# Maxima by query halves, spaced by TensorE's passes, in a four-layer attention kernel

## What is computed

```
xn = group_norm(x) * gn_w + gn_b
qkv = einsum('oc,bct->bot', qkv_w, xn) + qkv_b          # 8 heads: q, k, v of 32 channels
weight = softmax(einsum('bct,bcs->bts', q * scale, k * scale), axis=-1)
a = einsum('bts,bcs->bct', weight, v)
x = xn + einsum('oc,bct->bot', proj_w, a) + proj_b
```

## Time and profile before

| | us |
|---|---|
| three runs: median (lowest, highest) | 1786.18 (1785.3, 1792.4) |
| the profiled execution's own time | 1780.42 |
| its span, first to last instruction | 1778.6 |
| layers 0 and 1, and the prologue, to the first score of P0 | 613.9 |
| P0 to P14 (first score of P0 to that of P15) | 1087.0 |
| P15 and the end | 77.7 |

### The profile page before, as it was taken

One profiled execution on the slowest core, in us unless ns is written; L12 is line 12 of the kernel. 1 busy time (PEld: TensorE's weight loads), 2 busy tenths in 40 slices (PEclk: granted clock), 3 DMA queues, 4 the chain that ended last, 5 costly groups with the idle time before them and its releaser, 6 DMA issues.

```text
span 1778.6 us, 25007 instructions
## 1 busy us (share of the span) xinstructions
PE 1635.6 (92%) x8222; PEld 1004.7 (56%) x8222; DVE 1042.0 (59%) x1640; ACT 903.9 (51%) x1488; POOL 990.9 (56%) x394
## 2 busy tenths in 40 slices
PE   4888969999996899999999999999999999999987
PEld 2767758888884554554544545545455454454532
DVE  3665646455443776666765767567666576656621
ACT  3444415344341265565655666556556555555653
POOL 1222303122131187776886778678777687757785
PEclk7999989999997699999999999999999999999999
DMA  4000000000003113113031130330312303033000
GB/s 146 19 18 18 1 1 1 1 1 1 18 1 78 36 37 72 31 43 74 1 72 39 35 90 0 72 72 7 72 25 49 79 20 72 13 85 73 1 25 24
DMA packets 25085, 67.60 MB, mean 38 GB/s; under 512 B 7216, under 2 KB 9072, under 8 KB 24944
## 3 DMA queue, kind: packets, MB, share of 16 engines
q1 hardware_dynamic: 24944, 65.82, 15.1%
HBM read 7.82 MB, written 4.19 MB: 7 GB/s over the span
## 4 chain that ended last, share of the span: by engine, by line
PE 48%; DVE 8%; issue 4%; POOL 3%; DMA 2%; ACT 1%; SPq 1%; DVEq 0%; POOLq 0%; ACTq 0%
PE psO L954 12%; PE psD L89 11%; PE psD L1022 10%; PE psA L1049 7%; DVE BNS L1102 6%; PE psD L966 5%; POOL PA L1259 3%; PE psO L1049 3%; DMA QS<-MROW 2%; ACT PR L1212 1%; DVE sums_turned L1079 1%; DVE A L1083 1%; SPq L1286 1%; SPq L1288 0%; DVE A L1085 0%
## 5 line engine op out<-in xcount | busy, mean ns | idle before, releaser
L1102 DVE TENSOR_REDUCE BNS<-psD 128x1 f32<-128x512 f32 x1024 | 631.1, 681 | 180.7 <-PE psD L1022 180.6
L1259 POOL TENSOR_TENSOR PA<-PA,PR 128x2048 f32<-128x2048 f32 x128 | 585.7, 4576 | 14.2 <-ACT PR L1212 2.0
L1212 ACT ACTIVATE PR<-psA 128x512 f32<-128x512 f32 x688 | 396.3, 607 | 324.7 <-PE psA L1049 281.6
L1022 PE MATMUL psD<-KS,QS 96*128 96x512 f32 x1024 | 420.6, 445 | 17.3 <-DMA QS<-SL 10.8
L1049 PE MATMUL psA<-QS,KS 97*128 97x512 f32 x688 | 294.9, 437 | 40.6 <-DMA QS<-MROW 19.3
L1022 PEld LDWEIGHTS psD<-KS,QS 96*128 96x128 f32 x1024 | 198.9, 194 | 139.5 <-DVE BNS L1102 92.3
L1212 ACT ACTIVATE PR<-psO 128x512 f32<-128x512 f32 x336 | 203.8, 607 | 143.7 <-PE psO L1049 141.4
L680 POOL TENSOR_SCALAR P<-P,RS 128x1024 f32<-128x1024 f32 x64 | 71.8, 1122 | 360.1 <-DVE RS L398 360.1
L954 PE MATMUL psO<-PR,V 128*32 128x512 f32 x2048 | 246.4, 598 | 0.0
L1049 PEld LDWEIGHTS psA<-QS,KS 97*128 97x128 f32 x688 | 128.7, 190 | 179.6 <-issue 97.6
L1259 POOL TENSOR_TENSOR PA<-PR 128x2048 f32<-128x2048 f32 x32 | 146.4, 4576 | 146.1 <-PE psD L1022 127.6
(11 more groups left out here) (146 smaller groups left out, 2062.9 us busy)
## 6 DMA issues: line engine op xcount, KB each, us to landing
KS<-SH SPq DMA_DIRECT2D x128, 128.0 KB, 2.4
QS<-SH SPq DMA_DIRECT2D x128, 128.0 KB, 2.4
KS<-SL SPq DMA_DIRECT2D x64, 128.0 KB, 2.4
QS<-SL SPq DMA_DIRECT2D x64, 128.0 KB, 2.4
X<-x SPq DMA_DIRECT2D x4, 1024.0 KB, 9.2
out<-X SPq DMA_DIRECT2D x4, 1024.0 KB, 4.5
XN<-w SPq DMA_DIRECT2D x2, 768.0 KB, 8.5
KH<-KL SPq DMA_DIRECT2D x8, 128.0 KB, 2.3
```

The costliest lines, as they stand in the source:

```text
L1022: mm = e.matmul(full, QS[0:STACK, g, q, tile * PART:(tile + 1) * PART], KS[0:STACK, g, q, h * HALF:(h + 1) * HALF], start=True, stop=True)
L1102: top = e.tensor_reduce(MXH[:, h, q, tile:tile + 1], full, AX.X, ALU.max)
L1212: e.activation(PR[:, J % 4, (s % QUADH) * HALF:(s % QUADH + 1) * HALF], score_bank(s, p), ACT.Exp, scale=scale).then_inc(exp_done, 1)
L1259: e.tensor_tensor(PA[:, :], PR[:, (J - 1) % 4, :] if j == 1 else PA[:, :], PR[:, J % 4, :], ALU.add).then_inc(sum_done, 1)
```

## The change

- Maxima are made by **query halves**. `m` are the 32 of queries 0 to 511 of group G; `a` ("late") are the 32 of queries 512 to 1023. Six late ones of group G are made in the phase before it (`EARLY`), the other 26 in its own phase. `T` and `t` turn a half each, three units behind its last maximum (`LAG`). Step 0 waits for the first row, step 32 for the second. The prologue makes 38 maxima in place of 64, and P15 makes 26 where it had none.
- The times of the 64 maxima follow from TensorE's **passes**: `side_units` adds up what each step costs (`PASSES`) and places a maximum at every 64th part of the sum, so most now come as two to four in a step that has other long work, and steps with the score alone come two or three running.
- `WEIGH` moves its pairs to steps 11, 18, 26, 34, the sums `z` go from 34.9 and 2.9 to 36 and 4. `v`, `w`, `K`, `Q`, `p` move (`SIDE_AT`). The `x` operations go from steps 15 and 17 to 32 to 36, statistics are spread over steps 8.5 to 14.5, and the group means ride on `t`. GpSimd works out the factors and `input_low` between its two series of adds, and the low parts behind the second one.
- `QS` is laid out by query halves, so a copy to it has two runs of 2 KB for one of 4 KB. In the SP queue the stacks of group 1 stand ahead of the first row of group 0.

```
-        M_AT = (6, 58)
-        HOLES = [(35, 38)]
-        XN_AT = 12
-        HALVES_AT = {"v": (0, 1), "w": (3.5, 5), "K": (28, 29.3), "Q": (30.6, 31.9), "p": (14.5, 17.5, 20.5, 23.5),
-                     "z": (34.9, 2.9)}
+        EARLY = 6
+        LAG = 3
+        XN_AT = (32, 34, 36, 36)
+        BN_AT = (8.5, 10.5, 12.5, 14.5)
+        SIDE_AT = [{"v": (14.5, 21), "w": (23.5, 29.5), "K": (45, 47), "Q": (52.5, 54.5)},
+                   {"v": (5, 6.2), "w": (8.2, 9.4), "K": (45, 47), "Q": (52.5, 54.5), "p": (14.5, 29.5, 21, 23.5)}]
+        WEIGH = [(0, 11), (1, 11), (2, 18), (3, 18), (4, 26), (5, 26), (6, 34), (7, 34)]
+        PASSES = {"K": 6, "Q": 6, "v": 6, "w": 2, "z": 12, "p": 8}
+        Z_AT = (36, 4)
+        FIRST_AT = {"k": (0.1, 0.2), "q": (0.3, 0.4), "v": (1, 1.1), "w": (2, 2.1), "K": (8, 10), "Q": (12, 14)}
+        W3_AT = 28
...
+                load = [1] * STEPS
+                for u, ats in halves.items():
+                    for at in ats:
+                        load[-int(-at // 1)] += PASSES[u]
+                for _, at in WEIGH:
+                    for h in range(2):
+                        load[(at + STEPS // 2 * h) % STEPS] += QUADH
+                passed = [0] + list(accumulate(load))
+                for i in range(4 * ROWS):
+                    share = (i + 0.5) * passed[-1] / (4 * ROWS)
+                    s = [p <= share for p in passed].index(False) - 1
+                    ats.append(s - 1 + (share - passed[s]) / load[s])
...
-                        wait(e, row_dma, (P + 1) * 16)
                         for s in range(STEPS):
+                            if s % HALF_STEPS == 0:
+                                wait(e, row_dma, (2 * P + h + 1) * 16)
...
+                    def maxima(G, h):
+                        e.wait_ge(vec_free, units_taken(G + h, "Tt"[h]))
+                        e.dma_start(QS[STACK:STACK + 1, G % 2, h, :, :].rearrange("p q n -> p (q n)").bitcast(F32),
+                                    MROW[:, :].bitcast(F32)).then_inc(row_dma, 16)
+                    stack(0)
+                    stack(1)
+                    maxima(0, 0)
+                    for P in range(NGRP):
+                        maxima(P, 1)
...
+                        if P + 1 < NGRP:
+                            maxima(P + 1, 0)
+                        if P + 2 < NGRP:
+                            stack(P + 2)
```

More of the change, by code:

```diff
@@ L1 @@
 from contextlib import ExitStack
+from itertools import accumulate
 import concourse.bass as bass
@@ new lines, in side_units @@
+        def side_units(g, first=False, last=False):
+            early, late = (0 if last else EARLY), (0 if first and g == 0 else 2 * ROWS - EARLY)
+            tiles = ([("late", a) for a in range(2 * ROWS - late, 2 * ROWS)]
+                     + [("first", a) for a in range(0 if last else 2 * ROWS)] + [("late", a) for a in range(early)])
+            if first and g == 0:
+                halves, step = FIRST_AT, 1
+                ats = [6 + i for i in range(len(tiles))]
+            else:
+                halves, step = dict({} if last else SIDE_AT[g]), STEPS / (4 * ROWS)
+                halves["z"] = Z_AT
+                if first:
+                    del halves["p"]
+                load = [1] * STEPS
[6 more added lines that the diff above has]
+                passed = [0] + list(accumulate(load))
+                ats = []
+                for i in range(4 * ROWS):
+                    share = (i + 0.5) * passed[-1] / (4 * ROWS)
+                    s = [p <= share for p in passed].index(False) - 1
+                    ats.append(s - 1 + (share - passed[s]) / load[s])
+                step = 1
+            units = [(u, at, i) for u, at_halves in halves.items() for i, at in enumerate(at_halves)]
+            if first and g:
+                units = [x for x in units if x[0] != "z" or x[2] == 0]
+            for n, ((kind, a), at) in enumerate(zip(tiles, ats)):
+                units.append(("a" if kind == "late" else "m", at, a))
+                if a == 2 * ROWS - 1:
+                    units.append(("t" if kind == "late" else "T", ats[min(n + LAG, len(ats) - 1)] + 0.01, 0))
@@ L857, in units_taken @@
         def units_taken(G, u):
-            place, r = (G, None) if G < 2 else (2 + G % 2, G // 2 - 1)
+            place, r = (G, None) if G < 2 else (2 + G % 2, G // 2 - 1) if G < NGRP else (4, None)
             units = UNITS[place]
-            return base_of("vector", place, r) + taken(units, [x[0] for x in units].index(u) + 1, "vector")
-        WEIGH = [(0, 13), (1, 13), (2, 18), (3, 18), (4, 26), (5, 26), (6, 33), (7, 33)]
+            names = [x[0] for x in units]
+            return base_of("vector", place, r) + taken(units, len(names) - names[::-1].index(u), "vector")
         PIECES = NT - 1
@@ L1109, in take @@
                             take_half(full, p ^ i, i)
-                        elif u == "T":
-                            wait(e, row_dma, G * 16)
-                            e.tensor_scalar(MROW[:, :], full[0:QUADH * NT, 0:PART], -1.0, None,
+                        elif u in "tT":
+                            if u == "t" and norm is not None:
+                                e.tensor_copy(MV[:, :, :].rearrange("p t k -> p (t k)"), full[:, PART:PART + 2 * CT])
+                            wait(e, row_dma, (2 * G if u == "T" else 2 * P + 1) * 16)
+                            e.tensor_scalar(MROW[:, :], full[0:ROWS, 0:PART], -1.0, None,
                                             ALU.mult).then_inc(vec_free, 1)
@@ L1222, in factors @@
                     def factors(norm, place, r, layer):
-                        names = [u for u, _, _ in UNITS[place]]
-                        after = len(names) - names[::-1].index("s")
+                        after = [u for u, _, _ in UNITS[place]].index("t") + 1
                         e.wait_ge(vec_free, base_of("vector", place, r) + taken(UNITS[place], after, "vector"))
@@ L1242, in phase @@
                     def phase(P, p, G, g, place, r, layers, proj=None, norm=None, norm_b=None):
-                        if norm is not None and P is not None:
-                            squares(e, norm)
-                            factors(norm, place, r, layers[2])
                         if P is None:
@@ L1261, in phase @@
                                 if norm is not None and h == 0 and j == 3:
-                                    input_low(norm, norm_b, layers[2])
-                                if layers[0] != layers[1] and h == 0 and j == 3:
+                                    squares(e, norm)
+                            if norm is not None and h == 0:
+                                factors(norm, place, r, layers[2])
+                                input_low(norm, norm_b, layers[2])
+                                if layers[0] != layers[1]:
                                     e.wait_ge(w3_high, 1)
@@ L1277, in _, with stack @@
                     e.dma_start(WP[:, :, :], wp_dram[2]).then_inc(wp_loaded[2], 16)
-                    for G in range(NGRP):
+                    def stack(G):
                         g = G % 2
```

156 lines of the change are left out of this document (71 added, 85 removed).

## The result

The changed kernel takes 1793.1 us (median of 20 runs, 1790.4 to 1796.9), the kernel before 1785.3 (20 runs, 1777.0 to 1792.4). The ratio is 1.0044 with a 95% interval of 1.0033 to 1.0056: slower, by 7.8 us. The execution under the profiler took 1793.9 us with a span of 1792.1, where the one of before took 1780.4 with 1778.6. So the two profiles stand 13.5 us apart, the medians 7.8.

A forecast was written before the change was run, and what follows sets the result against it. TensorE was taken as the bound, losing 6.2 us per odd and 5.6 per even phase to row and VectorE waits. P0 +3.2, P1 to P14 +1.9, prologue -6.7, last phase +1.0: -0.6 on 1780.4; median 1786, range 1765 to 1810.

The forecast's parts named there:

- ScalarE's pace: Steps without side work run at exp's 0.49 us, costing TensorE 2.6 us in an odd phase, 2.7 in an even.
- The start: Prologue: fewer maxima, but K's eviction and stack(1)'s copies delay it; P0 starts at 607.2 instead of 613.9, -6.7 us.
- the loop entries: Three re-entries of the two loops keep their instruction-issue gap, 4.3 us each with half clock, 12.9 in all.
- Evictions: Maxima four units behind v, w, K or Q wait for ScalarE to empty banks: 3.0 us odd, 2.6 even.
- The second row: Odd phases, score 32: the row turned by t comes late, 1.25 us lost; hidden in even phases.
- P0: First phase: exp 32 waits for GpSimd's factors without output quarters as cover; 70.0 us against 66.8, +3.2.
- P15: Last phase, GpSimd-bound: 26 maxima put its first add 1.5 us later, one more ready score returns 0.5; +1.0 us.
- (a): Whole kernel: no change, within 9 us, as the forecast's own sum says; chance 0.40.
- (b): Eviction waits overlap ScalarE's pace and t's row comes in time, so faster: 1740 to 1775 us; chance 0.27.
- (c): GpSimd's adds, chained with exp, become the bound; even phases lose 3 us each with the next odd: 1807; chance 0.18.
- (d): More small waits in ten places of 14 phases, +35, or SP's queue holds t's row: 1805 to 1820; chance 0.11.
- (e): ScalarE-paced stretches bring the 0.95 clock everywhere, 3 us a phase, +45: 1830 us; chance 0.04.

The follow-up runs named there:

- e1_pieces: Changed kernel with only the pieces v, w, K and Q moved to other steps; 1767.0 us, 0.9907 of the kernel before.
- e6_half_exp: Changed kernel with exp over 256 of the 512 columns of each score, so its output differs; 1757.7 us, 0.9840 of the kernel before.
- e3_uniform: Changed kernel with one maximum per step instead of counting passes, and LAG = 1; 1783.8 us, 0.9986 of the kernel before.
- e5_ends: Changed kernel with P0's input operations four steps later and P15's second sum at step 3, maxima one per 0.8 step; 1796.7 us, 1.0070 of before.
- e4_start: Changed kernel with the prologue reordered: K and Q of group 1 behind T, first row's copy ahead of stack(1); 1781.1 us, 0.9976 of before.
- e10_holes: e3_uniform with six light steps behind the sums without a maximum and six weighting-pair steps with two; 1771.8 us, 0.9927 of before.
- e7_all: Changed kernel with the edits of e1_pieces (w placed differently), e4_start, P0 and P15 (maxima per 0.9 step), plus EARLY 7; 1747.1 us, 0.9793 of before.
- e8_steps: Changed kernel with maxima spaced by steps with six holes, EARLY 7, LAG 2, and v, w, K, Q moved; 1734.9 us, 0.9715 of before.
- e9_best: e8_steps plus the edits of the prologue, P0 and P15 (maxima one per 0.9 step); 1717.6 us, 0.9620 of before.

## Why the prediction was wrong

I forecast no change, and it is slower by 0.44%. The step that failed is the size of three terms of the sum: *ScalarE's pace* in the odd phase (2.6 us forecast, about 4.2 in P5), the eviction waits of P0 (put at nothing) and the first add of P15 (1.5 us later forecast, 2.9 measured). The mechanisms were those foreseen.

*The start* (607.2, measured 608.2) and *the loop entries* (three of 3.3 to 3.9 us of issue; with the half clock behind them some 14 us in place of 12.9) were near. In the start, each split copy to `QS` holds the queue 0.67 us where it was 0.64, about half a us for the 12 of a stack; I had taken nothing. At the three entries the gap stayed though the row no longer waits, so the row was not its cause. That it is the fetch of the branch's instructions is argued and not shown: the trace gives no releaser. The Trainium skill, page "Runtime: NRT & Kernel Launch", section "Instruction fetch mechanics", says that a taken branch whose target is outside the fetched window stalls until its page arrives; the three entries of 3.3 to 3.9 us fit that. That one entry of e1_pieces shows 0.17 with the same branch is left open. P6's weights (0.8) cost next to nothing: P6 takes 75.3, the even phases beside it 75.1 and 75.2.

*Evictions* (3.0 odd, 2.6 even) were about right. The brackets of P5 say 2.0 us (0.65, 0.50, 0.18, 0.66), but from start to start these four places lose 0.81, 0.66, 0.34 and 0.81: 2.6. In P6 it is 1.8; of the waits that I listed for it ahead of e1_pieces, the 0.34 is not one for an eviction. *The second row* (1.25) costs 0.84, counted the same way. *ScalarE's pace* (2.6) was put too low, and this outweighs the others: P5 lies 8.0 over the floor of 61.9, and less 2.6, 0.84 and 0.4 for the bursts some 4.2 are left for it. That figure is a remainder and includes errors of the floor. The starts of the scores show where most of it stands. Steps 5 to 10 and 37 to 42 lose 0.8 us each over their passes, as forecast, and steps 12 to 14 0.3 in place of 0.2. From step 59 of P5 to step 1 of P6 it is 1.5 in place of 0.8, with P6's first score waiting for exp (1045.45 above, 0.57). The rest, about 1, is spread over single steps that the forecast had at their passes, such as 25 (0.3). That exp is behind it is shown by e6_half_exp, where these waits are gone from P5, and, without touching exp, by e3_uniform. Over P1 to P14 the forecast is short by 6.8, with 1.2 of the entries.

*P0* (+3.2) took +5.8. The factor wait is there: ScalarE waits 4.71 us (5 forecast), TensorE 2.25 and 0.88.

```profile
646.77 0.50 PE L1069 MATMUL psO<-QS,KS 97*128 97x512 f32 x1 [2.25 <-ACT PR L1241]
...
648.38 0.50 PE L1069 MATMUL psA<-QS,KS 97*128 97x512 f32 x1 [0.88 <-ACT PR L1241]
```

A stretch of 3.4 us at half clock follows at 649.5 and costs 1.7. e5_ends brings 2.5 us back, in it this stretch. The eviction waits behind v0 and w0 (0.80, 0.27 and 0.25) are what I counted for even phases and left out of P0, where the same pieces lie at the same steps.

*P15* (+1.0) took +4.7. Its first add starts 12.0 us into the phase in place of 9.1, not 1.5 later: six maxima now stand ahead of the sum in its step, and each costs passes and a bank. GpSimd's adds carry that to the end. The other 1.7 us lie behind the last add, where the clock was low for longer: e4_start, with the same P15, took 80.8.

These errors make +14 us on the profiled execution (1.0 + 2.6 + 6.8 + 3.7), which is what it shows (1793.9 against 1780). They all have the same sign; the single costs put too high (evictions, row) are smaller than the one put too low.

*The step to the median* was wrong the other way: I added 5.8, as before, but the changed kernel's median stands 0.8 under its own profiled execution. Before, an execution may or may not meet short stretches at half clock, and its runs spread over 15 us; the changed kernel's spread over 6.5. That its median stands under the profiled execution is chance: one execution of a spread. So the forecast of the median, 1786 against 1793.1, looks better than the sum behind it, which is 14 off.

Of the rivals, (a)'s mechanisms held with larger sizes, and the 7.8 us are still within its 9; (b) is out, the eviction and row waits stand in steps of their own; (c) is out, since ScalarE waits for GpSimd's adds at one phase start alone (P7, 2.24 us) and P5 went to 65.6 with these adds unchanged; of (d)'s further small waits there is about 1 us a phase; (e) is out, packed phases still show 1.00. Its premise was misread besides: the clock of 0.95 in P15 of before is not that of the exp-paced steps but of 6.8 us at half clock from 1761.4 on, behind a wait of 4.33 us for GpSimd, and of the very end. For (e) the Trainium skill, page "TensorE: Matmul & The Clock Gate", section "A second HAM failure mode: psum-queue depth-cycling", describes swings of the clock by short pauses between groups of matmuls; no packed phase of the changed kernel shows them for pauses of 0.2 to 0.7 us, while e3_uniform and e10_holes show them behind single pauses of 1.0 to 1.4 us.

The belief behind the change failed as well: that maxima should be even in TensorE's passes. The engine that sets the light steps is ScalarE, and its time is even in steps.

## What to carry to other kernels

Spread side work by the time of the engine that sets the step, not by the busiest engine's own count: a matmul put where TensorE waits for exp is free, and the same matmul moved to a heavy step costs its full pass. With a ring of result banks drained by two engines, look at what stands one turn of the ring behind each unit of the slower or busier drainer; moving pieces so that a long group lies between was worth 1.8 us of 70. When a wait shrinks in the groups of waits, add up the others: 70 us left and over 100 came. And count a pause from start to start: the four eviction waits of P5 read 2.0 us in brackets and cost 2.6.

## What the runs showed of the hardware

A loop's entry can cost 2.9 to 4.5 us of issue or 0.17 with the same branch and nearly the same number of instructions: only the places of some of them differ (P3's entry in e1_pieces and e7_all against the rest).

From P0 to P14, in all thirteen profiles, every stretch at half clock (61 in all) begins during a wait of TensorE or at most 2.7 us behind it, and the shortest of these waits is 1.01 us: row waits, loop entries, waits for exp or VectorE. No phase of the changed kernel shows one for its pauses of 0.2 to 0.7 us. But such a wait need not bring one. Before, P1, P2 and P4 to P9 all begin with a row wait of 1.1 to 1.3 us; one of the eight had a stretch in one execution and three others in the next, some 1.6 us each. And P15 of e8_steps has a stretch, at 1701.7, with no pause over 0.31 us in the 8 us ahead of it.

What looks like noise of 15 us between runs was in part a property of that kernel's waits, as the changed kernel, with other waits, spreads over 6.5. It is no rule for the variants: e8_steps and e9_best spread over 1 us, e1_pieces and e7_all over 11, each with one run some 7 us over the next.
